# Cross attention: the score matmuls on two row tiles of 64 rows instead of one of 128

## The reference, cut to what matters

```python
xq  = layer_norm(x, qn_w, qn_b)
ctx = layer_norm(context, cn_w, cn_b)
q = (xq @ q_w).reshape(B, N, H, D)                       # B 2, N 2048, H 16, D 32
kv = (ctx @ kv_w).reshape(B, M, 2, H, D)                 # M 77
attn = jnp.einsum('bnhd,bmhd->bhnm', q, k) * scale
attn = softmax(jnp.where(xa_mask, neg, attn), axis=-1)
out = jnp.einsum('bhnm,bmhd->bnhd', attn, v).reshape(B, N, C) @ proj_w + proj_b
x = x + out
h = layer_norm(x, n2_w, n2_b)
return x + (gelu(h @ fc1_w + fc1_b) @ fc2_w + fc2_b)     # 2048 hidden channels
```

## Time and profile before

| | us |
|---|---|
| median of 3 runs | 1090.54 |
| lowest, highest | 1090.46, 1092.13 |
| the profiled execution | 1091.98 |
| its span | 1090.2 |
| TensorE busy (share of the span) | 1068.1 (98%) |
| VectorE busy | 824.1 (76%) |
| ScalarE busy | 513.2 (47%) |
| mean granted TensorE clock | 0.997 |

### The profile page before, as it was taken

One profiled execution on the slowest core, in us unless ns is written; L12 is line 12 of the kernel. 1 busy time (PEld: TensorE's weight loads), 2 busy tenths in 40 slices (PEclk: granted clock), 3 DMA queues, 4 the chain that ended last, 5 costly groups with the idle time before them and its releaser, 6 DMA issues.

```text
span 1090.2 us, 16741 instructions
## 1 busy us (share of the span) xinstructions
PE 1068.1 (98%) x5665; PEld 904.1 (83%) x5665; DVE 824.1 (76%) x1469; ACT 513.2 (47%) x1326; POOL 322.3 (30%) x243
## 2 busy tenths in 40 slices
PE   8999999999999997999999999999999999999998
PEld 6799999999899886888878788887888888888887
DVE  7888788888888787888787766677666668656655
ACT  4566565666655765454552433352343344223221
POOL 3344554444566637332603100301300020300000
PEclk9999999999999998999999999999999999999999
DMA  7011122111111049556186536244634533834322
GB/s 257 15 50 58 49 70 73 57 51 50 50 47 53 20 160 323 199 206 228 72 310 212 222 126 230 109 174 156 257 146 148 195 110 134 308 137 162 119 77 77
DMA packets 54894, 149.77 MB, mean 137 GB/s; under 512 B 13285, under 2 KB 21517, under 8 KB 46631
## 3 DMA queue, kind: packets, MB, share of 16 engines
q1 hardware_dynamic: 54239, 147.82, 37.6%
q10 hardware_dynamic: 584, 1.06, 0.3%
HBM read 108.39 MB, written 39.85 MB: 136 GB/s over the span
## 4 chain that ended last, share of the span: by engine, by line
PE 87%; DVE 7%; issue 2%; ACT 2%; DMA 1%; SPq 1%; DVEq 0%; ACTq 0%
PE bank L1841 30%; PE bank L1811 26%; PE bank L1684 8%; PE bank L1638 8%; PE bank L1669 6%; PE bank L1619 4%; PE bank L1651 2%; PE bank L1820 2%; DVE xTl L1186 2%; DVE ybuf L1433 1%; ACT xTh L846 1%; DVE acc L1446 1%; PE bank L1629 1%; PE bank L1601 1%; DVE hop L1406 1%
## 5 line engine op out<-in xcount | busy, mean ns | idle before, releaser
L1841 PE MATMUL bank<-w2r,gT 128*128 128x512 f32 x1536 | 361.2, 392 | 7.2 <-DVE acc L1446 7.0
L1841 PEld LDWEIGHTS bank<-w2r,gT 128*128 128x128 f32 x1536 | 287.6, 188 | 69.9 <-DVE acc L1446 10.0
L1811 PE MATMUL bank<-hop,w1r 128*128 128x512 f32 x1344 | 320.0, 396 | 0.0
L1811 PEld LDWEIGHTS bank<-hop,w1r 128*128 128x128 f32 x1344 | 251.4, 188 | 60.4 <-issue 0.3
L1446 DVE TENSOR_TENSOR acc<-bank,acc 128x512 f32<-128x512 f32 x256 | 176.8, 691 | 104.5 <-PE bank L1841 99.7
L1433 DVE TENSOR_TENSOR ybuf<-bank,ybuf 128x512 f32<-128x512 f32 x223 | 147.5, 688 | 80.8 <-PE bank L1811 74.8
L1053 ACT ACTIVATE ybuf<-ybuf,cols 128x512 f32<-128x512 f32 x127 | 91.2, 718 | 162.3 <-DVE ybuf L1433 162.3
L880 ACT ACTIVATE S<-S,nmax 128x77 f32<-128x77 f32 x256 | 89.2, 355 | 47.1 <-DVE nmax L1180 47.1
L1438 DVE TENSOR_TENSOR gT<-ybuf,gT 128x512 fp32r<-128x512 f32 x127 | 95.8, 774 | 0.0
L1046 ACT ACTIVATE ybuf<-bank 128x512 f32<-128x512 f32 x32 | 19.3, 602 | 156.0 <-PE bank L1811 156.0
L642 POOL TENSOR_TENSOR hrs<-hve,mhalf 128x1 f32<-128x1 f32 x32 | 18.5, 577 | 235.6 <-DVE hve L1416 235.6
(11 more groups left out here) (119 smaller groups left out, 1659.4 us busy)
## 6 DMA issues: line engine op xcount, KB each, us to landing
w1r<-w_scratch SPq DMA_DIRECT2D x24, 1792.0 KB, 7.2
w2r<-w_scratch SPq DMA_DIRECT2D x24, 1024.0 KB, 5.3
w_scratch<-w1r SPq DMA_DIRECT2D x8, 1792.0 KB, 6.7
xr<-in_x SPq DMA_DIRECT2D x16, 512.0 KB, 3.8
x_scratch<-xr SPq DMA_DIRECT2D x16, 512.0 KB, 2.8
hring<-x_scratch SPq DMA_DIRECT2D x32, 256.0 KB, 2.9
acc<-x_scratch SPq DMA_DIRECT2D x32, 256.0 KB, 3.9
w_scratch<-w2r SPq DMA_DIRECT2D x8, 1024.0 KB, 6.7
```

What stands on the lines that cost most here:

```text
L1811: mm = pe.matmul(bank_[:, :], w1r[:, w1_slot(s), c, w, kk * P:(kk + 1) * P], hop[i][:, d, kk, :], start=(kk == 0 and n == 0), stop=(kk == ...
L1841: mm = pe.matmul(bY[t % 2][:, :], gT[s % 2][:, j, d, t * P:(t + 1) * P], w2r[:, s % 2, j, w, :], start=(n == 0), stop=(n == 5))
```

## The change

The 128 rows of the array are used as two tiles of 64 rows (`tile_position` 0 and 64). Half 0 holds the first two heads of a group and half 1 the other two. The key block of a half has 2 x 77 = 154 columns, so `kbd` has 154 columns in place of 308. `score(t, pair)` now makes two groups at once: for each group and product one matmul on half 0 and one on half 1. The two halves write different banks: the bank of half 0 holds heads 0 and 1 of both groups (2 x 154 columns), the bank of half 1 heads 2 and 3. `masked(t, j)` takes one bank and writes its four heads to their old places in `S`. A pair waits until both banks are free, and both counts of `t_scores` come with its last two matmuls. Between other work the pairs stand where the couples of groups stood. In the preparation x_T(1) now stands before the second pair of tile 0 instead of within it. The memory map of everything else is unchanged.

```diff
-    kbd = [at(f"kbd{s}", [P, B, KT, GM], F32R) for s in "hl"]
+    kbd = [at(f"kbd{s}", [P, B, KT, 2 * M], F32R) for s in "hl"]
+    top[0] += 2 * B * KT * 2 * M * 4
...
+    HALF = 2 * D
...
-        v = kbd[part][h * D:(h + 1) * D, :, 2 * h2:2 * h2 + 2, h * M:(h + 1) * M]
+        v = kbd[part][h * D:(h + 1) * D, :, 2 * h2:2 * h2 + 2, (h % 2) * M:(h % 2 + 1) * M]
...
-            def masked(t, g_):
-                i = t * KT + g_
+            def masked(t, j):
+                i = t * KT + j
+                pair, half = j // 2, j % 2
...
-                dve.tensor_tensor(S[s.u][:, t, g_ * GM:(g_ + 1) * GM].rearrange("p (h m) -> p h m", h=HG),
-                                  s_bank(i, prep)[:, 0:GM].rearrange("p (h m) -> p h m", h=HG),
-                                  negm[:, s.u, t, :].unsqueeze(1).to_broadcast([P, HG, M]),
+                place = S[s.u][:, t, pair * 2 * GM:(pair + 1) * 2 * GM].rearrange("p (g h m) -> p g h m", g=2, h=HG)
+                dve.tensor_tensor(place[:, :, 2 * half:2 * half + 2, :],
+                                  s_bank(i, prep)[:, 0:GM].rearrange("p (g h m) -> p g h m", g=2, h=2),
+                                  negm[:, s.u, t, :].unsqueeze(1).unsqueeze(1).to_broadcast([P, 2, 2, M]),
                                   ALU.add).then_inc(v_scores.sem, 1)
...
-            def score(t, g_):
-                i = t * KT + g_
+            def score(t, pair):
+
+                i = t * KT + 2 * pair
+                if t == 0 and (prep is not None or pair == 0):
+                    v_q.wait(pe, s, pair if prep is not None else UT - 1)
+                v_scores.wait(pe, s, i + 1 - (2 if prep is None else 4))
                 if prep is None and i == 0:
-                    v_q.wait(pe, s, UT - 1)
-                if prep is not None and i in (0, 2):
-                    v_q.wait(pe, s, i // 2)
-                v_scores.wait(pe, s, i - (2 if prep is None else 4))
-                if prep is None and i == 1:
                     v_res.wait(pe, k.plus(-1), 0)
-                for n, (w, d) in enumerate(PRODUCTS):
-                    mm = pe.matmul(s_bank(i, prep)[:, 0:GM], qT[d][:, g_, t * P:(t + 1) * P], kbd[w][:, s.u, g_, :],
-                                   start=(n == 0), stop=(n == 2))
-                mm.then_inc(t_scores.sem, 1)
+                for g_ in range(2):
+                    for n, (w, d) in enumerate(PRODUCTS):
+                        for half in range(2):
+                            r = slice(half * HALF, (half + 1) * HALF)
+                            mm = pe.matmul(s_bank(i + half, prep)[:, g_ * 2 * M:(g_ + 1) * 2 * M],
+                                           qT[d][r, 2 * pair + g_, t * P:(t + 1) * P], kbd[w][r, s.u, 2 * pair + g_, :],
+                                           start=(n == 0), stop=(n == 2), tile_position=(half * HALF, 0))
+                            if g_ == 1 and n == 2:
+                                mm.then_inc(t_scores.sem, 1)
```

More of the change, by code:

```diff
@@ L1710, in step @@
                 score(0, 0)
+                x_T(1)
                 score(0, 1)
-                x_T(1)
-                score(0, 2)
-                score(0, 3)
                 values(0)
-                for g_ in range(KT):
-                    score(1, g_)
+                score(1, 0)
+                score(1, 1)
                 for m in range(KT):
@@ L1724, in step @@
                 score(0, 0)
-                score(0, 1)
             if front and prep is None:
@@ L1736, in step @@
             if scores and prep is None:
-                score(0, 2)
-                score(0, 3)
+                score(0, 1)
             if front:
@@ L1742, in step @@
                 score(1, 0)
-                score(1, 1)
             if front:
@@ L1748, in step @@
             if scores and prep is None:
-                score(1, 2)
-                score(1, 3)
+                score(1, 1)
             if back:
```

## The result

| | before | after |
|---|---|---|
| median, us | 1091.34 (4 runs, 1090.46 to 1093.31) | 1109.01 (4 runs, 1108.34 to 1110.85) |
| the profiled execution, us | 1091.98 | 1109.64 |
| its span, us | 1090.2 | 1107.8 |
| mean granted TensorE clock | 0.997 | 0.989 |

The changed kernel is slower: ratio 1.0158, 95% interval 1.0144 to 1.0173. That is 17.7 us by the medians and 17.6 by the spans of the two profiled executions. The forecast was 1104.8 us. It had the direction and the main cause, and was 4 us short. That nearness is partly luck: two terms were too large, and three places that had nothing in the sum made up for them and more.

What follows compares the result with a forecast made beforehand. TensorE's queue was taken to bound the kernel. Shape changes 25.8, less pair bodies 7.4 and the wait at q(0) 4.1, gave +14.3 us: 1106.3 for the profiled execution, 1104.8 as median; range 1089.0 to 1143.0.

Steps and rivals of the forecast that it cites:

- The pair's body: Twelve score matmuls of a pair: 0.73 us in place of 0.846, a gain of 7.4 us over 64 pairs.
- serial loads: Rival: weight loads of both tiles go one after another, pair body 1.31 us, +47.9 us, 1138.4 us; chance 0.20.
- The end of 0.65: Lower bound of a pair's body: loads of both tiles side by side, 6 x 0.109 = 0.65 us.
- The change of shape: Entering and leaving 64-row tiles around score matmuls: 0.20 and 0.21 us, together 0.41 for 63 stretches, 25.8 us.
- (a): First query projection q(0): TensorE's wait for VectorE's xTl shrinks by 0.29 us in 14 units, -4.1 us.
- (b): Last pair of a unit, score(1,1), needs both banks free: VectorE's masked(1,1) frees them in time, cost nothing.
- faster: Rival: shape change costs nothing, loads run side by side, body 0.65 us: -4.6 us, 1086 us; chance 0.11.
- (c): The wait for the residual, now in front of the whole first pair of a unit: cost nothing.
- (d): VectorE's two mask additions start only at the pair's end, up to 0.3 us later; 0.470 us each stays: nothing.
- (e): Preparation: smaller memsets and x_T(1) put ahead of score(0,1) cost nothing.
- no change: Rival: pair body 0.42 us plus shapes at 0.41, 0.83 against 0.846, about 1090 us; chance 0.07.
- slow short matmuls: Rival: short fp32r score matmuls at plain fp32 pace, 0.276 us each, +73 us, 1163 us; chance 0.05.

Runs made afterwards that it cites:

- columns78: The changed kernel with score matmuls on 78 of the 154 columns, leaving out the second head of each half: 1107.68 us, ratio 1.0146.
- waits_only: The kernel before, its 308-column matmuls on the full array, with the waits and counts of the change: 1098.35 us, ratio 1.0062.
- filled: The kernel before with 22 idle matmuls in TensorE's long wait at the start of the MLP: 1089.73 us, ratio 0.9986.
- extra128: The kernel before with one more 2-column matmul on the full array ahead of each couple of score groups: 1097.22 us, ratio 1.005.
- extra64: The kernel before with one more 2-column matmul on a 64-row tile ahead of each couple of score groups: 1110.33 us, ratio 1.0166.
- before_moved: The kernel before with three semaphore increments ahead of groups of matmuls in the first MLP block, moving the loop: 1103.8 us, ratio 1.0108.
- halves_in_turn: The changed kernel with all six matmuls of half 0 first, then the six of half 1: 1121.97 us, ratio 1.0275.
- after_moved: The changed kernel with three semaphore increments ahead of groups of matmuls in the first MLP block, moving the loop: 1105.7 us, ratio 1.0109.
- after_filled: The changed kernel with 28 idle plain fp32 matmuls in the wait at the MLP's start, also shifting its loop: 1101.49 us, ratio 1.0087.

## Why the prediction was right or wrong

The frame was right: what is added to TensorE's queue in a step is added to the kernel, save at the wait of q(0). The forecast for the attention phase was +14.3 us, measured were 11.5. The terms in their order:

**The pair's body: right in kind, 10% too dear.** The loads of both tiles run side by side and bound the pair; columns78 and the timeline show it. The 0.11 us that I had named as the sign of serial loads is the pace of couples; half of it, 0.056 us a load, is the pace I had given as mine. I had added a pace of issue of 0.061 us a matmul, from four one-row transposes, and said that no row shows TensorE go faster. That was a lower pace seen elsewhere, not a floor: couples leave 3 to 4 ns apart, and twelve matmuls take 0.66, not 0.73 us. The end of 0.65 that I worked out and passed over was the right value. Worth -4.5 us. The serial loads (+47.9) were ruled out by the same rows.

**The change of shape: right, a little too dear.** The two gaps at the one-row transposes carried over: 0.21 us until the first load, forecast 0.21; 0.31 us from the last couple to the first full matmul, forecast 0.295. Entering came out at 0.16 instead of 0.20 because a half-height matmul starts 0.07 us behind its load, not 0.11; leaving at 0.20 instead of 0.23. Together some -0.06 a pair. The Trainium skill (TensorEngine Tiling (Array Packing), Key Properties) says that a change of tiling mode drains the array and that tiles load and multiply in parallel; the trace is consistent with the first, with the next load only 0.21 us behind the last matmul's start at each end of a pair, and agrees with the second, with loads 3 to 4 ns apart.

**(a) The wait at q(0): right.** In step 7 the first pair shifts TensorE by 0.13 us, the second pair costs 0.18 more, and q(0) starts only 0.13 later: the second pair is hidden, as forecast, for 14 x 0.18 = 2.5 us instead of 4.1, because the pair itself was cheaper. What I said one would see was wrong, though: the wait was to be nearly gone, and it still reads 3.6 us in place of 4.5. The gap behind the pair now lies inside that idle time, and the profile gives the whole of it to VectorE.

**(b) The wait for both banks: right for this kernel, and thin.** The last pair adds 0.15 to 0.2 us in a step. waits_only shows 0.39 us in this very place for pairs that come earlier. A faster body would have run into it, as the rival "faster" said.

**(c) The wait for the residual: wrong.** "Nothing" was read from a step with layer norm. In the steps without it VectorE begins residual(0) a microsecond later, and the pair starts 0.25 us late on top: steps 1 to 4 and 13, 1.2 us. I had compared both kinds of steps for (b) and not for (c). The trace of before had the row, a wait of the fourth matmul for this residual.

**(d) and (e): right.** A mask addition takes 472 ns, before 470. The preparation and step 0 together grew by 1.2 us; their two units of pairs give 1.3. One sentence ahead of the prediction has to be corrected: in the preparation x_T(1) stands between the two couples of score groups in both kernels, so nothing moved there.

**Not in the sum.** The half-speed stretch in step 14: the step grew by 2.9 us, in waits_only, which waits there as well but at full clock, by 1.0; some 1.9 us, an estimate by difference. It came in all five kernels with the tiled pairs and in none with full-height scores. Why there, stays open: TensorE was busy 2.17 of 4 us before it, but waits_only shows as little (1.93 of 4, in a window a little earlier in its step) without it.

So the attention phase adds up: pairs 0.13 + 3 x 0.18 = 0.67 us a step, 16 steps 10.7; q(0) gives back 2.5; the residual 1.2; the half clock 1.9. Together 11.3, measured 11.5; with an uncertain half clock and up to 0.9 us of difference in the preparation, the last digit is luck. The sum on record has 14.3 for the pairs less q(0), where 8.2 were found: 6.1 too much. It has nothing for the residual and the clock, 3.1 too little, and nothing for the MLP, 6.2 too little.

**The MLP: missed altogether.** I wrote that the change doesn't touch the MLP. It adds 24 matmuls to each step of TensorE's program, and that shifts all code behind it. If a block holds 256 instructions, the MLP loop of some 1670 touches 7 blocks or 8, by where it begins:

| kernel | loop, in blocks | touched | branch, us | packets in the second pass |
|---|---|---|---|---|
| before | 25.0 to 31.5 | 7 | 0.23 | 0 |
| waits_only | 25.0 to 31.5 | 7 | 0.21 | 0 |
| filled | 25.2 to 31.7 | 7 | 0.23 | 0 |
| extra128 | 25.5 to 32.0 | border | 0.21 | 1 |
| extra64 | 25.5 to 32.0 | border | 3.37 | 8 |
| before_moved | 25.7 to 32.2 | 8 | 3.70 | 9 |
| after | 27.6 to 34.1 | 8 | 3.72 | 9 |
| halves_in_turn | as after | 8 | 3.70 | 9 |
| columns78 | as after | 8 | 3.59 | 9 |
| after_moved | 28.2 to 34.8 | 7 | 0.21 | 0 |
| after_filled | 28.0 to 34.5 | 7 | 0.21 | 0 |

The positions are counted from the program, with 256 instructions to a 16 KB packet. The packets bear the count out: up to the first jump back 31 had moved in the kernels whose loop ends in block 31, 32 in before_moved, 34 in those that end in block 34. The rule fits every clear case, in both directions, and I take the place of the loop as shown to be the cause: a loop over seven blocks was not fetched again, one over eight was. Why eight can't stay, no trace shows. The two border cases are the exception to think about. extra128 and extra64 execute the same number of instructions, yet only extra64 paid. The single packet of extra128 starts 1.8 us ahead of the loop's second jump back; extra64 fetched its 32nd packet 1.8 us ahead of the first. So extra64 had touched an eighth block when it jumped and extra128 had not, which fits the rule; what made the difference at the border stays open.

Of the rivals, "faster" and "no change" fell with the shape cost, which extra64 measured by itself, and "slow short matmuls" with the pace of 0.11 us: no record stands double within one half, and the 0.03 us that 76 columns fewer saved is the pace of full-size matmuls.

## What to carry over

Cutting a contraction into row tiles pays in full only while streaming is the bound. Here a load of 128 columns of fp32r weights took 0.11 us, nearly as long as streaming 256 columns (0.12), so at 154 columns the loads took over. Each stretch on another tile shape cost about 0.2 us at either end, so gather such matmuls into few long stretches. Alternate the tiles matmul by matmul: six and six in turn cost 13 us more. When a change adds instructions ahead of a long loop, look at the loop's jump back and the instruction queue in the profile after, and read a moved wait in every kind of step, not in one.

## What the runs showed of the hardware

- Loads and matmuls of two tiles of 64 rows go side by side, 3 to 4 ns apart; on one tile, loads of 128 fp32r columns follow each other after 0.11 us.
- A change of tile shape left a gap before the next load, at both ends. Going over to the tile, the load came 0.21 us after the start of a matmul of 256 columns and 0.33 after one of 512; going back, 0.20 to 0.21 us after the start of the last tiled matmul, whether it had 154, 78 or 2 columns (after, columns78, extra64).
- Matmuls on different row tiles don't keep the order of the program: in halves_in_turn half 1's second matmul starts 0.04 us before half 0's fifth and 0.15 before its sixth, which both stand ahead of it. The Trainium skill (TensorE: Matmul & The Clock Gate, Part 3, "What overlaps and what doesn't") says that matmuls start and end strictly in order, so that one increment on the last is enough. The measurement differs on the start and decides; ends are modelled in these traces. Who counts on one increment for two tiles should not rely on that sentence: the kernel here has one for each half.
- A jump back over a loop of some 1670 instructions took TensorE 0.21 or 3.7 us, by the loop's position; with the long one 8 or 9 packets of instructions moved in the pass behind it, with the short one none or one. In the changed kernel two gaps of 2.3 and 2.4 us and a half-speed stretch of 3.4 us lay behind it. The whole price in the MLP was from 2 us (extra64) to 8 (before_moved).
- The profile puts waits for instructions down to the engine whose semaphore stands at the instruction; the row of the weight load, with "issue", tells them apart.
